# Position products read queries kept column by column, with high and low parts stacked, in a two-block vision transformer kernel

## What is computed

```python
qkv = x @ qkv_w.T + qkv_b                       # 12 heads of 16 channels
r_q = q.reshape(b, NH, h, w, hd)
rel_h = jnp.einsum('bnhwc,hkc->bnhwk', r_q, Rh) # one table row set for each image row h
rel_w = jnp.einsum('bnhwc,wkc->bnhwk', r_q, Rw) # one for each image column w
attn = q @ k.T * scale + (rel_h[..., :, None] + rel_w[..., None, :])
```

## Time and profile before

| | us |
|---|---|
| median of 3 runs | 3370.66 (3368.36 to 3373.05) |
| profiled execution | 3370.78 |
| its span in the trace | 3368.9 |
| c0qkv, first part (position products begin at 97.3) | some 41 |
| c0qkv, position products to the first load of c0att | 97.3 to 195.6 |
| c1qkv, the same | 1288.2 to 1386.8 |

### The profile page before, as it was taken

The page is one execution under the profiler, slowest core; times in us unless marked ns, Lnnn a source line. Parts: engine busy times, 40 slices in busy tenths (PEclk is TensorE's granted clock), DMA queues, the critical chain, the costliest instruction groups (busy, mean ns, idle before and its releaser), DMA issues. The chain is left out here.

```text
span 3368.9 us, 62705 instructions
## 1 busy us (share of the span) xinstructions
PE 2764.8 (82%) x18708; PEld 1277.7 (38%) x18708; DVE 2414.6 (72%) x4597; ACT 1860.7 (55%) x2592; POOL 435.2 (13%) x513
## 2 busy tenths in 40 slices
PE   5948999997499239589999956199999959599999
PEld 3612222226499126222222234022222236366666
DVE  6458999974766354579999955589999835465665
ACT  4416777773255124167777736067777736465554
POOL 0010111111333510101111110201111100000000
PEclk9759999996699667599999977599999979699999
DMA  2555776664122214567766701101111110200000
GB/s 64 169 125 114 151 148 142 148 126 143 33 78 76 70 31 146 134 110 150 149 146 149 145 22 50 57 28 52 48 48 49 48 32 1 55 22 5 9 5 14
DMA packets 202070, 277.27 MB, mean 82 GB/s; under 512 B 54302, under 2 KB 93454, under 8 KB 201930
## 3 DMA queue, kind: packets, MB, share of 16 engines
q1 hardware_dynamic: 162346, 211.32, 27.1%
q0 software_dynamic: 19920, 31.57, 4.0%
q10 hardware_dynamic: 19664, 32.60, 3.3%
HBM read 196.93 MB, written 77.46 MB: 81 GB/s over the span
## 5 line engine op out<-in xcount | busy, mean ns | idle before, releaser
L750 DVE TENSOR_REDUCE c1att_mx<-c1att_m 128x1 f32<-128x512 f32 x768 | 493.4, 685 | 35.7 <-PE c1att_m L688 30.6
L750 DVE TENSOR_REDUCE c0att_mx<-c0att_m 128x1 f32<-128x512 f32 x768 | 493.4, 685 | 32.5 <-PE c0att_m L688 27.2
L750 DVE TENSOR_REDUCE f1att_mx<-f1att_m 128x1 f32<-128x512 f32 x768 | 493.3, 685 | 26.5 <-PE f1att_m L688 21.8
L996 ACT ACTIVATE c1att_p<-c1att_s 128x1024 f32<-128x1024 f32 x384 | 373.9, 1020 | 152.0 <-PE c1att_s L703 151.9
L996 ACT ACTIVATE c0att_p<-c0att_s 128x1024 f32<-128x1024 f32 x384 | 373.9, 1020 | 148.8 <-PE c0att_s L703 148.7
L996 ACT ACTIVATE f1att_p<-f1att_s 128x1024 f32<-128x1024 f32 x384 | 373.9, 1020 | 143.8 <-PE f1att_s L703 142.8
L1426 ACT ACTIVATE moe_h<-moe_u,moe_bu 128x512 f32<-128x512 f32 x192 | 136.5, 711 | 175.6 <-PE moe_u L1343 93.9
L688 PE MATMUL f1att_m<-f1att_km,f1att_qm 16*128 16x512 f16 x768 | 155.7, 401 | 88.6 <-DVE f1att_ka L959 52.9
L716 PE MATMUL f1att_o<-f1att_p,f1att_vs 128*32 128x512 f32 x1536 | 206.2, 609 | 0.6 <-ACT f1att_p L996 0.6
L716 PE MATMUL c0att_o<-c0att_p,c0att_vs 128*32 128x512 f32 x1536 | 206.2, 609 | 0.6 <-ACT c0att_p L996 0.6
L716 PE MATMUL c1att_o<-c1att_p,c1att_vs 128*32 128x512 f32 x1536 | 206.1, 609 | 0.6 <-ACT c1att_p L996 0.6
(11 more groups left out here) (608 smaller groups left out, 5430.8 us busy)
## 6 DMA issues: line engine op xcount, KB each, us to landing
xt<-rel_parts SPq DMA_DIRECT2D x256, 128.0 KB, 5.0
xt<-qk_parts SPq DMA_DIRECT2D x192, 128.0 KB, 4.4
y<-rel_parts SPq DMA_DIRECT2D x128, 128.0 KB, 5.6
y<-qk_parts SPq DMA_DIRECT2D x96, 128.0 KB, 5.1
c0att_qm<-rel_parts SPq DMA_DIRECT2D x144, 64.0 KB, 2.1
c1att_qm<-rel_parts SPq DMA_DIRECT2D x144, 64.0 KB, 2.1
expert_rows<-y SPq DMA_DIRECT2D x39, 192.0 KB, 2.0
o_sums<-c0att_o ACTq DMA_DIRECT2D x24, 256.0 KB, 4.3
```

The costliest lines, as they stand in the source:

```text
L750: dve.tensor_reduce(mx[:, n:n + 1], bank[:, :], AX.X, ALU.max).then_inc(s_mx, 1)
L996: act.activation(pr[h][kt % 2][:, :], sps[h][:, :], ACT.Exp).then_inc(s_e, 1)
```

## The change

Only the two `qkv` stages with position terms are touched.

- The three tiles `parts` are used again, as `by_x[g]`: once a chunk's matmuls are through (`s_v` at 4c + 4), GpSimd copies the 64 query rows of `high` into rows 0 to 63 of `by_x[g]` with image row and column exchanged, and VectorE copies those of `low` into rows 64 to 127. That is 24 copies of 64x512 on each engine. GpSimd's follow each chunk; VectorE's are placed one chunk late (`turn_low(c - 1)` after chunk c), so that the last six stand between the first part and its first `rlo`.
- The high table of the columns also goes to rows 64 to 127 (one ACT instruction more); the low one keeps zeros there.
- A column unit has 2 matmuls for each image column instead of 3: table high by (query high over query low), table low by the same. The moving operand is now runs of 16 neighbouring elements.
- PE waits for `s_byx` of group g before its column units, for `s_wh` 5, and for `s_zero` 4 in place of 5. GpSimd does one memset less.

```diff
+        by_x = parts
+        def by_columns(t, c):
+            return t[:, c * CHUNK:(c + 1) * CHUNK].rearrange("p (s x y) -> p s x y", s=2, x=QSIDE)
+        def by_rows(t, c, g):
+            return t[0:GW, at(c, g)].rearrange("p (s y x) -> p s x y", s=2, y=QSIDE)
...
+                for c in range(CHUNKS):
+                    pool.wait_ge(s_v, 4 * c + 4)
+                    for g in range(GROUPS):
+                        pool.wait_ge(s_hi, c * GROUPS + g + 1)
+                        pool.tensor_copy(by_columns(by_x[g][0:GW, :], c), by_rows(high, c, g)).then_inc(s_byx[0], 1)
...
+                        if k:
+                            for part in s_byx:
+                                pe.wait_ge(part, (CHUNKS - 1) * GROUPS + g + 1)
...
-                                pe.matmul(out, wh, row_of(top, k, r), start=True, stop=False)
-                                pe.matmul(out, wl, row_of(top, k, r), start=False, stop=False)
-                                ins = pe.matmul(out, wh, row_of(rest, k, r), start=False, stop=True)
+                                if k:
+                                    both = column_of(by_x[g], r)
+                                    pe.matmul(out, wh, both, start=True, stop=False)
+                                    ins = pe.matmul(out, wl, both, start=False, stop=True)
+                                    continue
...
+                def turn_low(c):
+                    dve.wait_ge(s_v, 4 * c + 4)
+                    dve.wait_ge(s_lo, c * GROUPS + GROUPS)
+                    for g in range(GROUPS):
+                        dve.tensor_copy(by_columns(by_x[g][GW:P, :], c), by_rows(low, c, g)).then_inc(s_byx[1], 1)
...
+                    if rel and c:
+                        turn_low(c - 1)
...
+                    turn_low(CHUNKS - 1)
...
+                        act.activation(th[1][GW:P, :], tab[1][:, :], ACT.Identity).then_inc(s_wh, 1)
...
-    return q.rearrange("p (n s y x) -> p s x n y", s=2, y=QSIDE, x=QSIDE)[:, r // QSIDE, r % QSIDE]
+def column_of(q, r):
+    return q.rearrange("p (n s x y) -> p s x n y", s=2, x=QSIDE, y=QSIDE)[:, r // QSIDE, r % QSIDE]
```

More of the change, by code:

```diff
@@ L277, in qkv @@
         s_rel, s_rhi, s_rlo = m.sem("rel"), m.sem("rhi"), m.sem("rlo")
+        s_byx = [m.sem(f"byx{k}") for k in range(2)]
         s_rst = [[m.sem(f"rst{k}{u}") for u in range(2)] for k in range(2)]
@@ L345, in _ @@
                 pool.wait_ge(s_init, 2)
-                for i, t in enumerate(th + tl if rel else ()):
+                if not rel:
+                    return
+                for i, t in enumerate((th[0], tl[0], tl[1])):
                     pool.memset(t[GW:P, :], 0.0).then_inc(s_zero, 1)
                     pool.wait_ge(s_zero, i + 2)
+                for c in range(CHUNKS):
[3 more added lines that the diff above has]
+                        pool.tensor_copy(by_columns(by_x[g][0:GW, :], c), by_rows(high, c, g)).then_inc(s_byx[0], 1)
             @block.tensor
@@ L384, in _ @@
                 pe.wait_ge(s_tabs, 2)
-                pe.wait_ge(s_zero, 5)
+                pe.wait_ge(s_zero, 4)
+                pe.wait_ge(s_wh, 5)
                 pe.wait_ge(s_vt, TILES)
@@ L399, in _ @@
                                 out = row_bank(rp[qq % 4], k, j)
-                                pe.matmul(out, wh, row_of(top, k, r), start=True, stop=False)
-                                pe.matmul(out, wl, row_of(top, k, r), start=False, stop=False)
-                                ins = pe.matmul(out, wh, row_of(rest, k, r), start=False, stop=True)
+                                if k:
[3 more added lines that the diff above has]
+                                    continue
+                                pe.matmul(out, wh, row_of(top, r), start=True, stop=False)
+                                pe.matmul(out, wl, row_of(top, r), start=False, stop=False)
+                                ins = pe.matmul(out, wh, row_of(rest, r), start=False, stop=True)
                             ins.then_inc(s_rel, 1)
@@ L492, in _, with row_of @@
                     store_rel(act, GROUPS - 1, 1, qq // 2, qq % 2, 0, rhi)
-def row_of(q, k, r):
-    if k == 0:
-        return q.rearrange("p (b u s y x) -> p u y b s x", b=B, u=2, s=2, y=QSIDE)[:, r // QSIDE, r % QSIDE]
-    return q.rearrange("p (n s y x) -> p s x n y", s=2, y=QSIDE, x=QSIDE)[:, r // QSIDE, r % QSIDE]
+def row_of(q, r):
+    return q.rearrange("p (b u s y x) -> p u y b s x", b=B, u=2, s=2, y=QSIDE)[:, r // QSIDE, r % QSIDE]
+def column_of(q, r):
+    return q.rearrange("p (n s x y) -> p s x n y", s=2, x=QSIDE, y=QSIDE)[:, r // QSIDE, r % QSIDE]
 def row_bank(bank, k, j):
```

## The result

Measured against the kernel before, run beside it: 3336.53 us median (3334.91 to 3349.32, 5 runs) against 3372.59 (3368.36 to 3375.49, 5 runs), ratio 0.9901 with a 95% interval of 0.9881 to 0.9921. That is some 36 us less, where 53 were forecast; 3336.5 lies inside the stated range of 3300 to 3350, 18.5 us above the forecast itself. The profiled execution has a span of 3334.3 us; before it was 3368.9.

A forecast was written before the change was run, and what follows sets the result against it. PE was taken to bound the column units, then stores: 49.7 us per layer from the units shrinks to 26.4 because of stores, copies and small edits cost 0; two layers, 3370.8 - 52.8 = 3318.0 us, range 3300 to 3350.

The forecast's parts named there:

- the case that the forecast rests on: Copies on POOL (GpSimd) and DVE (VectorE) run side by side at no cost to the sum; 3318 us, chance 0.52.
- PE bounds the column units, and the layout is why: Position products: operand in runs cuts matmuls from 230 to 55 ns, units from 2.79 to 0.72 us; alone 49.7 us per layer.
- The third product, the small edits: Column units: 8 matmuls at 55 ns, 0.44 us at full clock; extra ACT instruction, one memset less, changed waits: cost 0.
- Stores take part of the gain back: Before attention: 72 position stores remain from 131.2, 34.6 us at 273 GB/s; attention at 169.2, 26.4 us earlier per layer.
- The wait of ACT at g = 2: ACT stops until g = 0 stores land at 141; its last stores land by 165, hidden by stores ending at 166.8.
- The copies: First part: DVE's 24 copies at 0.69 us, POOL's 24 at 0.9; first part grows some 3 us, effect on sum 0.
- the rival in which they take turns: First part: POOL's and DVE's copies exclude each other, 8.2 us per chunk; attention at 175 to 176, 3331 us, chance 0.15.
- The cover that I named for the copies: DVE's longer first part and delayed first `rlo` lie in SP's shadow, SP being 29 us late there.
- SP's issue as the bound: Position stores: SP's issue at 0.91 us each, not DMA engines, limits; 15.0 us per layer, 3341 us, chance 0.12.
- Stores hidden after all: Rival: stores take nothing back, full 49.7 us per layer saved; 3271 us, chance 0.07.
- the layout no help: Rival: column units' 230 ns come from something else, only the third product goes, 22 us; 3327 us, chance 0.08.
- GpSimd as the bound: Rival: POOL's copies hold up the column units, slower than before from 4.2 us per copy; to 3406 and more, chance 0.06.

The follow-up runs named there:

- e3: Changed kernel with high over low parts stacked but not turned: straight copies, column products still read every 16th element, two products; 3347.41 us, ratio 0.9913.
- e4: Changed kernel with a third matmul in each column product (the one with the low table issued twice); 3341.42 us, ratio 0.9899.
- e1: Changed kernel without GpSimd's 24 copies per stage and without PE's wait for them; 3337.85 us, ratio 0.9889.
- e6: Changed kernel with query and key part stores issued as 64 rows and GpSimd's copies placed after the first part; 3273.69 us, ratio 0.9716.
- e10: Changed kernel without VectorE's 24 copies per stage and without PE's wait for them; 3337.79 us, ratio 0.9887.
- e9: Changed kernel with GpSimd's copies after the first part and after VectorE's copies, group by group, a repeat run; 3337.43 us, ratio 0.9885.
- e5: Changed kernel with DRAM axes of query and key parts reordered, each store issued as 64 rows, not 4 by 16; 3297.79 us, ratio 0.9789.
- e7: Kernel before the change with query and key part stores issued as 64 rows, not 4 by 16; 3345.09 us, ratio 0.9925.

## Why the prediction was right or wrong

The kernel got faster by two thirds of what was forecast, and the time lies in the range. But the case that the forecast rests on, copies that cost nothing, is not what happened: the range was wide enough to hold its rivals too. What follows takes the steps one by one.

*PE bounds the column units, and the layout is why.* Right. 55 ns for 230 with the operand in runs, and 230 again in e3.

*The third product, the small edits.* A third product would have cost nothing (e4). The small edits weren't tried by themselves; no wait for them shows in the changed kernel's trace.

*Stores take part of the gain back.* Right, and it is the main term. By the forecast's own working 49.7 us per layer were to be had from the units alone; 18 came. Three sizes in this term can be read from e1, which is the forecast's case without turn-taking. SP's first position store: 131.2 forecast, 132.73 measured, with 24 high stores issued by then, as forecast. The rate at first: I added 1 us for SP being alone; 12 us at 234 GB/s instead of 273 are 2 us, and ACT came back at 144.8, not 141, so the second queue joined later. The end: 169.2 forecast, 173.8 measured. The step was right and its size 4.6 us short.

*The wait of ACT at g = 2.* Right in kind, and longer than drawn (19.3 us in e1). In the changed kernel it disappears, since everything before it is late.

*The copies.* This step failed. VectorE's copy alone is 0.61 us, under the 0.69 I took; GpSimd's alone is 1.11, within its bounds and above my 0.9. But they don't run alone. The likeliest case, that they run side by side, had 0.52 and was wrong; the rival in which they take turns had 0.15 and is what happened, with the sign that was named for it, a first part beyond 112 (115.9). Its bill was drawn somewhat too high for the first part (8.2 us per chunk, 60 / 8 = 7.5 measured). Its end looks right, attention at 175 to 176 forecast and 177.1 measured, but that is luck: two errors nearly cancel. It had SP at its first position store at 137, and SP was there at 128.26. It kept the forecast's 72 stores for what is left from there, though position products that start 19 us later leave ACT no time to issue 24 of them: the trace has 3 high stores issued by then, so 93 were left. They are 12.2 MB, 43 us at 282 GB/s, where the rival's sum has 34.6. The cover that I named for the copies was the right one. SP was late anyway and only came to its position stores at 128.26; that is why 16 us lost in the first part cost 3 to 4 us at the end.

*Why no more than 36 us.* Against the forecast's stage of 122.2 us (attention at 169.2, first load at 47.0) the first layer has 130.1: 4.6 us are the size of the store term as e1 has it, 3.3 are what the first layer takes beyond e1, the price of turn-taking. The second layer is of the same kind (131.6). The rest of the program is 2.4 us longer, within what two profiles of one kernel differ by.

*SP's issue as the bound.* Its 3341 is nearer to the measured 3336.5 than my 3318, and in the changed kernel the 48 position stores of SP do take 44.8 us, 0.93 each, as in that rival. But they wait for the DMA engines, which are at a share of 0.90 there: in e1, with less of ACT's traffic beside them, the same 48 take 37.1 us, 0.77 each, under the 0.91 that the rival needs.

*Stores hidden after all, the layout no help, GpSimd as the bound.* None of them happened; GpSimd's copies at 1.46 us are far from the 4.2 at which they would have decided.

## What to carry to other kernels

Before speeding up a producer, ask what its results wait for next: here 18 of an estimated 50 us per layer came, and 36 once the stores of query and key parts were spread over all engines and GpSimd's copies moved (e6). Reordering the axes of one DRAM tensor was worth as much again as the change itself (ratio 0.9901 to 0.9789), though of the 41 us that it takes off the three stages 28 come from the third attention's, which the change doesn't touch. Work put on GpSimd "because it is idle" wasn't free here, since VectorE was copying in SBUF or reading two SBUF tensors at the same time. And when a cost sits in the shadow of another bound, measure it twice, once with that bound removed: the same placement of copies was worth 3 to 4 us per layer and then 12.

## What the runs showed of the hardware

- A half-precision moving operand of 128 columns at a step of 32 bytes takes 230 ns where one in runs of 16 takes 55, at a granted clock of 1.00; at 0.50 it takes the same.
- A GpSimd copy and a VectorE subtraction of two SBUF tensors delay each other: 0.68 us alone, up to 1.6 beside it (e10), and the ends of the two alternate. A VectorE copy of 64x512 with a step of 32 bytes on its read side takes 0.61 us alone (e1) and 0.885 on average in the changed kernel, up to 1.5 where it meets one of GpSimd's. VectorE instructions with one operand in PSUM kept their time, 0.35 and 0.69 us. For the subtraction this is what the Trainium skill says ("SBUF — State Buffer", "SBUF: two separate sides"), which the prediction held to be open; for a copy it names a 2-port mode, and no run here shows which mode the copy ran in.
- For GpSimd the same copy takes 1.11 us alone, and one follows another every 1.06, 2.1 ns per element (e9).
- A store of 128 KB whose DRAM side is 4 by 16 rows is issued every 1.28 us, with four or five packets under way; as 64 rows it is issued every 0.63 us with mostly 12 to 16 under way (e5, e7).
